# A routed feed-forward kernel on one core: a third row buffer for every batch, router logits turned by transposes, and POOL's memsets only in slots 32 to 63

## The reference

```python
# cond layer, for each of 16 batches of 512 tokens, D = 512, rank 16
z1 = einsum('bfi,bir->bfr', x, v) / 512
z = einsum('bfr,bor->bfo', z1, u) / 16
g = gelu(x @ W.T + fc_bias + z + b)          # exact gelu
# routed feed-forward, 8192 tokens, 16 experts of 128 hidden units, top 4
prob = softmax(g @ w_router + b_router)
mask = is_among_top4(prob)
h = relu(einsum('nd,ebd->neb', g, w1b) + b1b)
y = einsum('neb,ebd,ne->nd', h, w2b, mask) + b2
out = x + y
```

## Time and profile before

| what | value |
|---|---|
| median of 3 runs | 1146.56 us (1144.09 to 1147.14) |
| profiled execution, its own time | 1149.37 us |
| its span, first to last instruction | 1147.6 us |
| mean granted TensorE clock | 0.89 |
| busy: PE, DVE, ACT, POOL | 75%, 75%, 51%, 63% |

### The profile page before, as it was taken

The page is one execution under the profiler, slowest core; times in us unless marked ns, Lnnn a source line. Parts: engine busy times, 40 slices in busy tenths (PEclk is TensorE's granted clock), DMA queues, the critical chain, the costliest instruction groups (busy, mean ns, idle before and its releaser), DMA issues.

```text
span 1147.6 us, 18685 instructions
## 1 busy us (share of the span) xinstructions
PE 865.1 (75%) x4893; PEld 682.7 (59%) x4893; DVE 861.7 (75%) x2175; ACT 581.1 (51%) x1061; POOL 727.4 (63%) x1038
## 2 busy tenths in 40 slices
PE   8989989999999999999999876999999930000000
PEld 7757767777777776777777655788888820000000
DVE  4556666777687767767778974878998759987777
ACT  6535545756676575657657753766667610000000
POOL 1588888888888888888888897555555530000000
PEclk9989989999999999999999997999999965555555
DMA  6798679988899888988778887689987589999999
GB/s 188 262 330 299 236 270 334 310 293 298 288 314 305 289 285 300 312 282 297 265 276 313 302 289 262 245 296 342 317 282 243 192 313 425 425 427 429 426 432 378
DMA packets 103241, 354.88 MB, mean 309 GB/s; under 512 B 29961, under 2 KB 29961, under 8 KB 92384
## 3 DMA queue, kind: packets, MB, share of 16 engines
q1 hardware_dynamic: 59616, 217.22, 55.0%
q0 software_dynamic: 43424, 136.37, 30.3%
q10 hardware_dynamic: 96, 0.10, 0.0%
HBM read 200.47 MB, written 169.65 MB: 323 GB/s over the span
## 4 chain that ended last, share of the span: by engine, by line
PE 50%; DVE 14%; POOL 12%; DMA 11%; issue 7%; ACT 3%; another core or an unknown queue 2%; ACTq 0%; POOLq 0%; DVEq 0%; SPq 0%
PE lay L1185 12%; DMA w2l<-yt 9%; PE yps L1327 9%; PE hid L1294 8%; PE trn L1279 7%; POOL yt L563 4%; POOL xg L544 4%; PE hid L1299 4%; POOL w2l L528 3%; DVE stx L1040 3%; PE hid L1171 2%; PE trn L1206 2%; ACT gsb L643 2%; DMA outT<-ys 2%
## 5 line engine op out<-in xcount | busy, mean ns | idle before, releaser
L544 POOL DMA_INDIRECT xg<-grow,ix x224 | 226.7, 1012 | 70.2 <-issue 36.4
L817 DVE TENSOR_TENSOR gsb<-trn,gsb 128x512 fp32r<-128x512 f32 x239 | 162.4, 687 | 127.3 <-ACT gsb L643 75.2
L563 POOL DMA_INDIRECT yt<-ys,ids x170 | 176.7, 1039 | 72.6 <-issue 35.8
L1185 PE MATMUL lay<-w2l,xs 128*128 128x512 f32 x768 | 194.3, 403 | 0.0
L1279 PE MATMUL trn<-idf,gr 128*128 128x128 f32 x956 | 147.3, 277 | 27.0 <-DVE gsb L817 12.9
L1185 PEld LDWEIGHTS lay<-w2l,xs 128*128 128x128 f32 x768 | 144.6, 192 | 30.1
L528 POOL MEMSET w2l<- 128x320 f32 x412 | 161.3, 392 | 0.1
L1279 PEld LDWEIGHTS trn<-idf,gr 128*128 128x128 f32 x956 | 115.8, 142 | 68.3 <-DVE gsb L817 22.9
L643 ACT ACTIVATE gsb<-trn 128x512 fp32r<-128x512 f32 x239 | 142.6, 597 | 26.5 <-PE trn L1279 15.2
L1294 PE MATMUL hid<-gsb,w1c 128*128 128x512 f32 (+1 forms) x576 | 133.1, 374 | 11.9 <-ACT gsb L643 10.2
L671 ACT ACTIVATE hv<-hid,b1c 128x512 f32<-128x512 f32 (+1 forms) x94 | 52.6, 584 | 155.4 <-PE hid L1299 53.0
(11 more groups left out here) (243 smaller groups left out, 1823.9 us busy)
## 6 DMA issues: line engine op xcount, KB each, us to landing
gr<-xg SPq DMA_DIRECT2D x49, 1056.0 KB
xs<-yt SPq DMA_DIRECT2D x16, 2048.0 KB, 19.5
w2l<-yt SPq DMA_DIRECT2D x15, 2048.0 KB, 19.5
gr<-xg SPq DMA_DIRECT2D x45, 528.0 KB
stx<-xT SPq DMA_DIRECT2D x64, 256.0 KB, 4.3
outT<-ys SPq DMA_DIRECT2D x31, 512.0 KB, 20.4
xg<-xrow SPq DMA_DIRECT2D x16, 528.0 KB
w2f<-xrow SPq DMA_DIRECT2D x16, 512.0 KB
```

Of the source, the lines that this page charges most:

```text
L544: pool.indirect_dma_start(out=xg, out_offset=bass.IndirectOffsetOnAxis(ap=ix[:, row_buffer(b), q, k:k + 1], axis=0), in_=grows[row_buffer( ...
L563: pool.indirect_dma_start(out=yt, out_offset=bass.IndirectOffsetOnAxis(ap=ids[:, j % 8, c:c + 1], axis=0), in_=yss[result_buffer(j)][:, c, ...
L817: dve.tensor_tensor(gsb[:, :, LO, c * P:(c + 1) * P], turned[TURN_BANK[n]][:, :].rearrange("p (k t) -> p k t", k=KC), gsb[:, :, HI, c * P: ...
L1185: pe.matmul(lay[s % 2][:, :], xs[:, b % 2, k, h, cols], wls[:, k, a, :], start=(k == 0 and a == HI and h == HI), stop=False)
```

## The change

`row_buffer(b)` becomes `b % 3` for all batches, and the third buffer `grow3` lies in the back part of `w2l`. `yspare` goes, and the result buffers are given out anew (five of them; two until tile 33). The waits of the first tiles for the third row buffer go; the presplit of expert 11 and of those behind it gets one for `grow3` instead. The logits are turned by four transposes of 128 x 128, and DVE adds the four partial sums with a reduction of its own into `lexp`; `sumk` and its setup on POOL go. `rest` does nothing outside slots 32 to 63 and writes 288 floats there. `stop` is left out for the last three tiles. In slots 33 to 66 POOL sends the results first and writes the rows behind them (before: in every fourth slot only). The presplits stand in slots 67 to 74 in plain order.

```diff
-SPARE = 40
-MORE = 36, 39, 43, 55
+MORE = 34, 36, 39, 55
-REST = 320
+REST = 288
 def row_buffer(b):
-    return b % 3 if b < 6 else b % 2
+    return b % 3
...
-        free = [0, 1] + [2] * (j <= SPARE) + [3] * (j >= MORE[0])
-        free += [4] * (MORE[1] <= j < MORE[3]) + [5] * (MORE[2] <= j < MORE[3])
+        free = [0, 1] + [2] * (MORE[0] <= j < MORE[3]) + [3] * (j >= MORE[1]) + [4] * (MORE[2] <= j < MORE[3])
...
-        yspare = nc.alloc_sbuf_tensor_at("yspare", [P, 4, D], F32, offset=w2l_at + 8 * D * 4)
+        grow3 = nc.alloc_sbuf_tensor_at("grow3", [P, 4, W], F32, offset=w2l_at + 11 * D * 4)
...
-        yss = (ys[:, 0, :, :], ys[:, 1, :, :], yspare, stx, grow[:, 0, :, 0:D], grow[:, 1, :, 0:D])
+        yss = (ys[:, 0, :, :], ys[:, 1, :, :], grow[:, 1, :, 0:D], stx, grow[:, 0, :, 0:D])
...
             def rest(s):
+                if s < LAG + 2 or s >= SLOTS:
+                    return
                 if paced[0] > 0:
                     pool.wait_ge(g_pace, paced[0])
-                idle = w2l[:, NE - 1, 0:REST].bitcast(F32) if s < SLOTS + 7 else rep[:, :, :].rearrange("p q e -> p (q e)")
-                pool.memset(idle, 0.0).then_inc(g_pace, 1)
+                pool.memset(w2l[:, NE - 1, D - REST:D].bitcast(F32), 0.0).then_inc(g_pace, 1)
                 paced[0] += 1
...
-                if j + LAG + 2 < PACED:
-                    rest(j + LAG + 2)
-                elif c == 1:
+                rest(j + LAG + 2)
+                if j + LAG + 2 >= PACED and c == 1 and j < NTILE - 3:
                     stop()
...
-                first = s <= LAG + 2 or q != 3
+                first = s <= LAG + 2 or SLOTS + 3 <= s
...
-                for n in presplit_in(s):
-                    presplit_w2(PRESPLIT[n])
+                if SLOTS + 3 <= s < SLOTS + 3 + NE // 2:
+                    for e in range(2):
+                        presplit_w2(2 * (s - SLOTS - 3) + e)
...
             def choose(b):
-                lgs = rps[:, 256:256 + 4 * NE].rearrange("p (q e) -> p q e", q=4)
+                lgs = lexp
                 dve.wait_ge(p_lt, b + 1)
-                step(dve.tensor_reduce(lmax[:, :], lgs, AX.X, ALU.max))
+                step(dve.tensor_reduce(lgs[:, :, :], rps[:, :].rearrange("p (q k e) -> p q e k", q=4, k=KC)[:, :, 0:NE, :],
+                                       AX.X, ALU.add))
+                step(dve.tensor_reduce(lmax[:, :], lgs[:, :, :], AX.X, ALU.max))
...
                 if e == NE - 1:
-                    dve.wait_ge(g_pace, 4 * SLOTS + 4 * (SLOTS + 5 - LAG))
-                if e == 8:
-                    dve.wait_ge(s_y[2], results_sent(max(j for j in range(NTILE) if result_buffer(j) == 2)))
+                    dve.wait_ge(g_pace, 8 * (SLOTS - LAG - 2))
+                if e == 11:
+                    for q in range(4):
+                        dve.wait_ge(s_sc[2][q], rows_sent(NB - 2))
...
-                pe.wait_ge(g_s, KC + 1)
                 for q in range(4):
-                    last = pe.matmul(rps[:, 256 + q * NE:256 + (q + 1) * NE], lgT[:, q * P:(q + 1) * P], sumk[:, :],
-                                     start=True, stop=True)
+                    last = pe.transpose(rps[:, q * P:(q + 1) * P], lgT[:, q * P:(q + 1) * P], idf[:, :])
```

More of the change, by code:

```diff
@@ L36 @@
 AHEAD = EARLY + 8
-REST = 320
+REST = 288
 PACED = SLOTS + 13
-PRESPLIT = [*range(8), *range(12, NE), *range(8, 12)]
 ALU = mybir.AluOpType
@@ L109, in result_buffer @@
     return RESULT_BUFFER[j]
-def presplit_in(s):
-    n = 2 * (s - SLOTS - 3)
-    if s > SLOTS + 8:
-        n -= 4
-    return range(n, n + 2) if SLOTS + 3 <= s < SLOTS + 13 and s not in (SLOTS + 9, SLOTS + 10) else ()
 def results_sent(j):
@@ L213, in adaln_ffn @@
         wrz = sb("wrz", [P, KC, 2 * NE], F32)
-        sumk = sb("sumk", [P, NE], F32)
         lmax = sb("lmax", [P, 4], F32)
@@ L291, in adaln_ffn @@
         s_sc = [[sem(f"s_sc_{n}_{q}") for q in range(4)] for n in range(3)]
-        s_y = [sem(f"s_y_{n}") for n in range(6)]
+        s_y = [sem(f"s_y_{n}") for n in range(5)]
         s_yin = [sem(f"s_yin_{n}") for n in range(len(yin))]
@@ L435, in _ @@
                 if s == SLOTS + 16 + 8:
-                    for n in (4, 5):
+                    for n in (2, 4):
                         sp.wait_ge(s_y[n], results_sent(max(i for i in range(NTILE) if result_buffer(i) == n)))
@@ L1016, in result @@
                     dve.wait_ge(p_r, SLOTS // 2)
-                elif result_buffer(j) > 3:
-                    b = NB - 6 + result_buffer(j)
+                elif result_buffer(j) > 1:
+                    b = NB - 5 + result_buffer(j)
                     for q in range(4):
                         dve.wait_ge(s_sc[row_buffer(b)][q], rows_sent(b))
-                if j == 1 or (j == 0 and c == 3):
-                    for q in range(4):
-                        dve.wait_ge(s_sc[2][q], rows_sent(5))
                 dve.tensor_copy(yss[result_buffer(j)][:, c, :], second_out[RESULT_BANK[4 * j + c]][:, :]).then_inc(v_y, 1)
@@ L1125, in _ @@
                         take_tile(j + 1, c)
[L1126 to L1127 removed]
+                    if SLOTS + 3 <= s < SLOTS + 3 + NE // 2 and c % 2 == 0:
+                        presplit_w2(2 * (s - SLOTS - 3) + c // 2)
                     if s <= SLOTS and 0 <= j - 1 and c % 2 == 1 and c < chunks(j - 1):
```

35 lines of the change are left out of this document (12 added, 23 removed).

## The result

The change makes the kernel slower: 1218.3 us (median of 4 runs, 1213.22 to 1222.26) against 1146.76 us of the kernel before on the same chip, a ratio of 1.063 (95% interval 1.0575 to 1.0678). The forecast was 1133.3 us with a range up to 1153 us. The profiled execution took 1213.22 us, with a span of 1211.4 us.

A forecast was written before the change was run, and what follows sets the result against it. PE was taken to bound the fused stretch, POOL next. Terms -7.2 - 1 - 3.5 - 1.6 = -13.3 us took the profile from 1149.4 to 1136.1 us, median 1133.3 us; 8-in-10 range 1119 to 1153 us.

The forecast's parts named there:

- POOL's memsets: Fewer, shorter memsets on POOL: it follows the routing without falling behind by a batch; -1 us (0 to -4).
- the stall of 4.66 and 5.08 us: PE idle at half clock behind the layers, no releaser named by the trace; left as it is in the forecast.
- Rival A: Slower: transposes at the turned logits let PE's clock fall to half in more places; 1163 us, chance 0.12.
- Rival B: Slower: unpaced row writes delay loads of x in the layers' stage; +5 us net, 1151 us, chance 0.12.
- Turned logits: Transposes replace sumk matmuls, saving PE 0.63 us a batch; -7.2 us, between 0 and -10.1.
- Third row buffer and order of sends: Row and result buffers, sends before row writes in slots 33 to 66: price 0, hidden by PE's work.
- Behind the layers: Presplit 15's wait for the last memset goes, four presplits move into tiles; net -3.5 us (-5 to -1.5).
- Last stops: POOL's stops in the last sends, tiles 69 and 70, cost about 0.8 us each; removing them gives -1.6 us.
- within 2 us of the copy's end: Sign at tile 0: its first send starts no more than 2 us after its copy ends.
- The fused stage is 5.5 us shorter: Sign for slots with layers and one tile each, 205 to 586 us before: shortens by 4 to 6 us.
- C: No change: DVE waits take back PE's savings, another wait is uncovered, only stops stay; 1144 us, or 1147, chance 0.17.
- the first 150 us get longer: Sign in the layers' stage: if this start of the kernel lengthens, the forecast is wrong.

The follow-up runs named there:

- f1_after_again: The changed kernel run again, nothing altered, on a 1148 us chip: 1213.53 us, 1.056 of the kernel before.
- f2_early_again: The changed kernel with 288-float memsets also in slots 0 to 31, run again on a 1148 us chip: 1153.96 us, ratio 1.003.
- e3_sumk: The changed kernel with the four sumk matmuls in place of the transposes and the added reduction: 1223.69 us, ratio 1.066.
- g2_before_turned: The kernel before with only the logits turned by transposes and the added reduction, on a 1130 us chip: 1132.25 us, ratio 1.001.
- e2_late: The changed kernel with memsets also in slots 64 to 76, none in slots below 32: 1202.84 us, ratio 1.048.
- h2_all42_again: The changed kernel with memsets up to slot 76 (80 floats from slot 71) and the fifth result buffer from tile 42, 1148 us chip: 1136.6 us, ratio 0.988.
- e4_before_noearly: The kernel before with its memsets left out in slots 0 to 31 and nothing else changed: 1208.87 us, ratio 1.053.
- e1_early: The changed kernel with 288-float memsets also in slots 0 to 31, first run, 1148 us chip: 1157.31 us, ratio 1.006.
- e7_stop2: The changed kernel with a four-float memset and a wait for it behind every second row write below slot 32, 1130 us chips: 1109.94 us, ratio 0.982.
- e6_small: The changed kernel with 80-float memsets added in slots below 32, on a 1130 us chip: 1106.88 us, ratio 0.979.

## Why the prediction was wrong

**The step that failed is the one on POOL's memsets.** It said that without them "POOL follows the routing and no longer falls behind by a batch" and took -1 us (0 to -4). The first half is what happened: POOL issues a batch's sixteen writes at 1.27 us and then waits for the next lists (121.2 us in nine waits, the longest of 38.1 us). What I didn't price is what the writes do to others. On the 1148 us chips the early memsets are worth 59.6 us (`f1_after_again` against `f2_early_again`) and, taken from the kernel before alone, 60.7 us. My bound on it was made from POOL's own times and from PE's idle time from 155 to 205 us; neither row could show a cost that only appears when the spacing goes. The spacing itself was mis-sized too: I took 1.14 us a write without its memset, the gap "issue" staying at 0.17 us, and it is 1.27 us, as the gap grows to 0.30 us. A sign of the cost was in the rows, and I left it "as it is": the stall of 4.66 and 5.08 us. Of the two, only the first has no releaser on PE; the second waits for ACT, whose own waits there are "remote". It stands where the kernel before has its short memsets (slots 71 to 76): its sends come 1.33 us apart there (702.17 and 703.50 us).

**Rival A**, the clock. The half clock is real (0.84 in the layers' stage), but it follows the holes, and it comes without the new transposes too (`e3_sumk`). `g2_before_turned` with them is at 1.001. By the rule of the Trainium skill ("TensorE: Matmul & The Clock Gate", Part 4) that I had weighed for A, the transposes should have cost clock. Neither run shows a loss by them, so here the measurement decides against it as a reason.

**Rival B**, DMA. It had a part of the right place (50 to 150 us; the loss goes on up to the first copy at 247.3 us) and the wrong mechanism. That it said slower is luck, and its price (5 us) is under a tenth of the 71.5 us by which the medians differ. The DMA engines are less busy in the slow kernel.

**Turned logits**, -7.2 us. The sizes were right (9.4 us of weight loads, a reduction of 0.42 us), the value was not: alone it gives nothing (1.001, 0.999 to 1.003, on a 1130 us chip). In the changed kernel `e3_sumk` is at 1.066 (1.061 to 1.070) against 1.063 (1.0575 to 1.068): the intervals overlap, so a gain of some us is possible and not shown. What failed here is "I count the full 0.63 us for the eight fused batches". On the 1130 us chips the fused stage was not PE's alone, as the wait for row writes in `g2_before_turned` shows. On the 1148 us chips that wait is 3.2 us, and why no gain shows there is open: with sumk the changed kernel's fused stage is 391.9 us and without it 392.5, and 5 us are less than two profiles of one kernel differ by.

**Third row buffer and order of sends**, 0. Off to both sides on the 1130 us chips: 10.3 us gained in the fused stage (with the shorter memsets, and not told apart from them), 10.7 us lost behind it, where the fifth result buffer brings a wait that my list of the edits never priced, since I looked at tiles before 34 only. On the 1148 us chips that wait shows in `e2_late` (28.7 us), and with the buffer given out later the stage behind the layers of `h2_all42_again` takes 142.3 us, as before. In the changed kernel itself it is hidden, as that stage is late anyway.

**Behind the layers**, -3.5 us. The wait of presplit 15 is gone, as said, but the stage is 10.9 us longer. The unnamed stall of the earlier trace rows is twice as long (9.15 and 9.28 us), and that stage lost its memsets as well. `e2_late`, which has them, has no such stall there, but as its wait for the fifth buffer stands in the place, the memsets are not shown to be what removes it.

**Last stops**, -1.6 us. The last stage went from 418.8 to 418.2 us. Not tested apart; it is within what the same stage varies in runs on these chips (417.9 to 420.4 us).

**The signs.** Tile 0 is sent 253.60 - 247.32 = 6.3 us after its first copy began, before 12.4. I had said within 2 us of the copy's end, and it is 5.7 us, so that is a miss. The fused stage is 5.5 us shorter (4 to 6 forecast), but this hit is luck: `e4_before_noearly`, with neither the transposes nor the third buffer, is 10.7 us shorter there, and `e1_early`, with both, 0.3 us. (C's price has a slip: 1146.6 - 1.6 is 1145.0, not 1144.) The sign "the forecast is wrong if ... the first 150 us get longer" was the one that told.

**What stays open**: why PE's completions are seen late while POOL issues indirect DMAs. The runs show that it depends on what stands between the writes and on the chip. They speak against the transposes, which `e3_sumk` does without, and against the DMA engines' load, which is lower in the slow kernels. Whether it is the pause or the memset's own work was not separated on a chip where it matters (`e7_stop2` ran on the 1130 us chips alone). How one hinders the other no trace of this case shows. The Trainium skill ("DMA: Bandwidth & Descriptors", Latency and other measured facts) gives contention at the ports of the descriptor rings of such DMAs as a best guess, called not certain, for something else: why two of the 16 DMA engines are usually slower than the others. No run here tests whether that bears on this one.

## What to carry to other kernels

A pause that does no work may be what keeps the other engines' waits short: before taking pacing out of a queue of indirect DMAs, take it out alone and look at the other engines' waits, not at the queue's. When a profile shows several engines idle at once with waits for a finished instruction and no releaser, ask what another engine issues in that stretch. And a buffer that is handed out to a new use must be followed to the last transfer that leaves it: one number of `MORE` was worth 17 to 20 us, more than the whole gain that was forecast.

## What the runs showed of the hardware

- On the 1148 us chips, indirect DMAs of POOL with 128 rows of 2112 bytes, issued each 1.27 us with nothing between, go with starts 8.5 and 12.3 us late of what waits for TensorE in the hole shown, and taking the memsets between them away costs 59.6 and 60.7 us. With a memset of 288 floats behind each, 1.48 us apart, the loss is all but gone (ratio 1.003).
- Chips differ in how much of this they bear: 1.31 us between the writes is 3.7% slower than before on a 1148 us chip and 2.1% faster on a 1130 us chip. With 1.48 us the same two kinds stand at 1.003 and, with extra loads, 0.991. Behind the layers, at 1.29 us with no memsets, the trace of `f2_early_again` (1148 us chip) has 34.4 us of "remote" waits on ACT and that of `e6_small` (1130 us chip) none.
- The kernel before takes 1.6% less time on the 1130 us chips. From the copy of tile 45 to the end, a run there takes 412.2 to 415.5 us, on the others 416.6 to 420.4.
